# The image reloaded into dead slots of X before the barrier, corner matrices earlier, squares added on GpSimd

## What is computed

```python
x = x + gelu(layernorm_over_channels(selective_scan(groupnorm(x))) * lnw + lnb)   # "x + conv"
t = tokens(x)                                     # (4, 1024, 192)
t = t + attention(layernorm(t), qkv_w, qkv_b, proj_w, proj_b, bias_table)
t = t + experts(layernorm(t), ...)
```

## Time and profile before

| | us |
|---|---|
| median of 3 runs | 2855.5 (2854.14 to 2861.66) |
| the profiled execution | 2855.03 |
| its span in the trace | 2853.3 |
| end of `scan` (last DVE product) | 1412.84 |
| first `val` of `mid` | 1446.84 |
| last `low_part` of `mid` | 1552.12 |
| start of attention (POOL memset) | 1555.27 |

### The profile page before, as it was taken

The page is one execution under the profiler, slowest core; times in us unless marked ns, Lnnn a source line. Parts: engine busy times, 40 slices in busy tenths (PEclk is TensorE's granted clock), DMA queues, the critical chain, the costliest instruction groups (busy, mean ns, idle before and its releaser), DMA issues. The chain is left out here.

```text
span 2853.3 us, 33000 instructions
## 1 busy us (share of the span) xinstructions
PE 2263.2 (79%) x8796; PEld 805.0 (28%) x8796; DVE 2096.6 (73%) x2852; ACT 1333.5 (47%) x1870; POOL 1407.1 (49%) x726
## 2 busy tenths in 40 slices
PE   3676667665666666666678899999999879999999
PEld 1111111111111111111143123232332236766767
DVE  4999999999999999999655887786878551212212
ACT  3444445445454454445445276675767532222221
POOL 3999999999999999999545000000000110000000
PEclk9577766777676776767778799999999879999999
DMA  4544544554454445445327013112313330000000
GB/s 119 175 142 172 175 144 156 177 170 150 145 180 162 152 158 176 154 146 176 124 62 161 1 25 46 25 25 30 41 25 42 75 82 6 6 6 6 6 6 11
DMA packets 101853, 274.04 MB, mean 96 GB/s; under 512 B 17089, under 2 KB 32007, under 8 KB 101639
## 3 DMA queue, kind: packets, MB, share of 16 engines
q1 hardware_dynamic: 97600, 271.89, 32.7%
q10 hardware_dynamic: 4078, 0.19, 0.1%
HBM read 226.55 MB, written 41.22 MB: 94 GB/s over the span
## 5 line engine op out<-in xcount | busy, mean ns | idle before, releaser
L686 POOL TENSOR_TENSOR hs<-hs,c_rep 128x1024 f32<-128x1024 f32 x384 | 897.5, 2355 | 80.1 <-DVE hs L782 49.9
L472 PE MATMUL psU<-b_stack,b_sel 96*128 96x512 bf16 x640 | 312.1, 500 | 449.7 <-DVE hs L782 447.0
L1732 DVE TENSOR_REDUCE mx<-ps 128x1 f32<-128x512 f32 x864 | 539.2, 682 | 108.4 <-PE ps L1571 98.1
L1707 ACT ACTIVATE P<-ps 128x512 f32<-128x512 f32 x768 | 417.7, 599 | 239.5 <-PE ps L1583 215.4
L732 DVE TENSOR_TENSOR psU<-psU,dtu_rep 128x512 f32<-128x512 f32 x640 | 428.2, 674 | 28.5 <-PE psU L472 13.1
L601 ACT ACTIVATE decay<-dt_rep,a_neg 128x1024 f32<-128x1024 f32 x320 | 360.5, 1140 | 164.1 <-DVE hs L782 141.9
L440 PE MATMUL psY<-hs,state_sel 128*32 128x512 f32 x1572 | 424.8, 902 | 4.8 <-ACT du L578 3.5
L782 DVE TENSOR_TENSOR_SCAN hs<-decay,hs,psU 128x512 f32<-128x512 f32 x320 | 406.6, 1271 | 2.3
L782 DVE TENSOR_TENSOR_SCAN hs<-decay,psU 128x512 f32<-128x512 f32 x320 | 386.2, 1207 | 0.0
L1571 PE MATMUL ps<-ks,qs 96*128 96x512 bf16 x864 | 345.3, 403 | 24.4 <-DVE mx L1732 9.9
L472 PEld LDWEIGHTS psU<-b_stack,b_sel 96*128 96x128 bf16 x640 | 62.5, 100 | 977.8 <-DVE hs L782 875.6
(11 more groups left out here) (235 smaller groups left out, 2357.7 us busy)
## 6 DMA issues: line engine op xcount, KB each, us to landing
c_rep<-bc_rows SPq DMA_DIRECT2D x132, 512.0 KB, 4.6
dt_rep<-dt_rows SPq DMA_DIRECT2D x99, 512.0 KB, 4.5
dtu_rep<-dt_rows SPq DMA_DIRECT2D x99, 512.0 KB, 6.2
b_rep<-bc_rows SPq DMA_DIRECT2D x33, 512.0 KB, 6.0
dt_rows<-dt SPq DMA_DIRECT2D x33, 384.0 KB, 3.3
dt_rows<-soft SPq DMA_DIRECT2D x33, 384.0 KB, 3.4
qs<-qk_parts SPq DMA_DIRECT2D x90, 128.0 KB, 6.6
ks<-qk_parts SPq DMA_DIRECT2D x90, 128.0 KB, 7.2
```

The lines of the kernel that those rows point to most:

```text
L472: pe.matmul(psU[:, q % UR, :], s.b_sel[:, r, nq, :], b_stack[:, p, CH * pos:CH * pos + CH], start=True, stop=True).then_inc(b_spread, 1)
L686: pool.tensor_tensor(h, h, c_rep[:, nq, :], ALU.mult).then_inc(hc_ready, 1)
L1707: nc.scalar.activation(P[:, kt % 2, head, :], ps2[:, bank, :], ACT.Exp).then_inc(exp_done, 1)
L1732: v.reduce_max(mx[:, slot, u:u + 1], ps1[:, (slot * MAXES + u) % R, :], AX.X).then_inc(max_done, 1)
```

## The change

- `X` lives on through `mid` and `attention`. SP loads batches 0 and 1 of x into slots 1 and 2 of `X` (`raw_slot`) behind the last loads of the scan loop, in front of the barrier. `raw` and `Z` are gone: the normed batches go to slots 0 and 3 (`z_slot`).
- At the start of `mid` SP issues the table rows first, then the weights, and then batches 2 and 3 of x as soon as `add_x(0)` and `add_x(1)` have run.
- On DVE `add_x(0)` runs ahead of the copies of the projection weights; the two corner instructions run behind these copies, ahead of the first `centre`. On POOL the mask of the corners runs ahead of the first `add_squares`.
- The split of the corners moves from iteration 2 to iterations 5, 6 and 7 in pieces, the copies by SP from iteration 7 to iteration 12.
- At the end of the scan POOL adds the two halves of the squares for m = 1 to 5 (`tail_squares`: two ahead of `add_y`, three behind it), and `tail_variance` needs one matmul in place of two there.

The core of the diff (renamings of the same indices are left out):

```diff
@@ -48,6 +48,14 @@
+
+def raw_slot(b):
+    return 1 + b % 2
...
+
+def load_x(sp, w, s, b):
+    sp.dma_start(s.X[:, raw_slot(b), :, :], w.x[b].rearrange("(f p) h w -> p f (h w)", p=HC)).then_inc(s.x_in[b % 2], 16)
@@ -489,11 +497,15 @@
                 def tail_variance(m):
-                    pe.wait_ge(t_squared, m + 1)
...
                         pe.wait_ge(t_log, m - 1)
-                    for f in range(2):
-                        t = pe.matmul(psU[0:HC, m % 2, :], s.average[:], tail_work(m)[:, f, :], start=(f == 0), stop=(f == 1))
+                    if m == 0:
+                        pe.wait_ge(t_squared, 1)
+                        for f in range(2):
+                            t = pe.matmul(psU[0:HC, m % 2, :], s.average[:], tail_work(m)[:, f, :], start=(f == 0), stop=(f == 1))
+                    else:
+                        pe.wait_ge(t_summed, m)
+                        t = pe.matmul(psU[0:HC, m % 2, :], s.average[:], tail_work(m)[:, 0, :], start=True, stop=True)
@@ -715,7 +727,16 @@
                                 pool.sem_inc(alone, 1)
+                def tail_squares(m):
+                    pool.wait_ge(t_squared, m + 1)
+                    q = tail_work(m)
+                    pool.tensor_tensor(q[:, 0, :], q[:, 0, :], q[:, 1, :], ALU.add).then_inc(t_summed, 1)
+
+                tail_squares(1)
+                tail_squares(2)
                 add_y(NB * UNITS - 1, NB * UNITS // 2 - 1, NB - 1, UNITS - 1)
+                for m in range(3, TAIL_STEPS):
+                    tail_squares(m)
@@ -893,6 +914,8 @@
                         load_c(nu, 3)
+                for b in range(2):
+                    load_x(sp, w, s, b)
@@ -1025,8 +1048,6 @@
 
-        Z = sb("Zq", [HC, 2, 2, L])
-        raw = sb("raw", [HC, 2, 2, L])
@@ -1072,11 +1092,14 @@
 
-        def half(t, c, ring):
-            return t[:, c // 2 % ring, :, CH * (c % 2):CH * (c % 2) + CH]
+        def half(t, b, c):
+            return t[:, b, :, CH * (c % 2):CH * (c % 2) + CH]
+
+        def z_slot(b):
+            return 3 * (b % 2)
...
         def norm_out(kind, c):
-            return half(Z, c, 2) if kind else half(s.Y, c, NB)
+            return half(s.X, z_slot(c // 2), c) if kind else half(s.Y, c // 2, c)
@@ -1087,30 +1110,24 @@
             def _(sp):
-                def load_x(b):
-                    sp.dma_start(raw[:, b % 2, :, :], w.x[b].rearrange("(f p) h w -> p f (h w)", p=HC)).then_inc(x_in[b % 2], 16)
...
 
-                sp.dma_start(w_rows[:], w.qkvw.rearrange("(m p) d -> p m d", p=HC)).then_inc(w_in, 16)
-                load_x(0)
-                sp.dma_start(p_rows[:], w.projw.rearrange("(m p) d -> p m d", p=HC)).then_inc(p_in, 16)
...
                 sp.dma_start(hankel[:].rearrange("p e h -> p (e h)"), win).then_inc(tab_in, 16)
+                sp.dma_start(w_rows[:], w.qkvw.rearrange("(m p) d -> p m d", p=HC)).then_inc(w_in, 16)
+                sp.dma_start(p_rows[:], w.projw.rearrange("(m p) d -> p m d", p=HC)).then_inc(p_in, 16)
...
                 sp.dma_start(vb[:], w.qkvb[2 * D:3 * D].rearrange("(o d) -> o d", o=1).broadcast_to([128, D])).then_inc(vb_in, 16)
-                load_x(1)
+                for b in (2, 3):
+                    sp.wait_ge(x_added, 2 * (b - 1))
+                    load_x(sp, w, s, b)
...
                     c, m = x // MT, x % MT
-                    if i == 1:
-                        for late in (2, 3):
-                            sp.wait_ge(x_added, 2 * (late - 1))
-                            load_x(late)
@@ -1121,7 +1138,7 @@
                                 sp.dma_start(rows[19 * part:19 * part + 19, :], pick[:, k, :]).then_inc(corner_in, 16)
-                    if i == GROUPS + 1:
+                    if i == 2 * GROUPS:
@@ -1162,12 +1179,12 @@
                     add_halves(c, 1, c)
+                pool.wait_ge(corner, 2)
+                pool.affine_select(out=corners[:, 0, :, :], in_=corners[:, 0, :, :], compare_op=ALU.is_ge, fill=0.0, base=0,
+                                   pattern=[[0, HEADS], [1, 19]], channel_multiplier=-1).then_inc(corner, 1)
...
                 add_halves(2, 1, 2)
-                pool.wait_ge(corner, 2)
-                pool.affine_select(out=corners[:, 0, :, :], in_=corners[:, 0, :, :], compare_op=ALU.is_ge, fill=0.0, base=0,
-                                   pattern=[[0, HEADS], [1, 19]], channel_multiplier=-1).then_inc(corner, 1)
@@ -1319,16 +1336,17 @@
                 def add_x(b):
-                    v.wait_ge(x_in[b % 2], 16 * (b // 2 + 1))
+                    v.wait_ge(s.x_in[b % 2], 16 * (b // 2 + 1))
...
                     for c in range(2):
-                        y = half(s.Y, 2 * b + c, NB)
-                        v.tensor_tensor(y, half(raw, 2 * b + c, 2), y, ALU.add).then_inc(x_added, 1)
+                        y = half(s.Y, b, c)
+                        v.tensor_tensor(y, half(s.X, raw_slot(b), c), y, ALU.add).then_inc(x_added, 1)
...
                 v.memset(scl[:, 2:3], 1.0).then_inc(own_v, 1)
+                add_x(0)
@@ -1336,7 +1354,12 @@
                 t.then_inc(padded, 1)
-                add_x(0)
+                v.wait_ge(tab_in, 16)
+                v.wait_ge(last_in, 16)
+                v.tensor_copy(corners[:, 0, :, :], hankel[:].rearrange("p e h -> p h e")[:, :, ::-1]).then_inc(corner, 1)
+                v.wait_ge(corner, 1)
+                v.tensor_tensor(corners[:, 0, :, :], corners[:, 0, :, :], last_row[:].unsqueeze(2).broadcast_to([19, HEADS, 19]),
+                                ALU.subtract).then_inc(corner, 1)
@@ -1344,12 +1367,6 @@
                 t.then_inc(w_taken, 1)
-                v.wait_ge(tab_in, 16)
-                v.wait_ge(last_in, 16)
-                v.tensor_copy(corners[:, 0, :, :], hankel[:].rearrange("p e h -> p h e")[:, :, ::-1]).then_inc(corner, 1)
-                v.wait_ge(corner, 1)
-                v.tensor_tensor(corners[:, 0, :, :], corners[:, 0, :, :], last_row[:].unsqueeze(2).broadcast_to([19, HEADS, 19]),
-                                ALU.subtract).then_inc(corner, 1)
@@ -1381,16 +1398,16 @@
                         add_x(LAST)
-                    if i == 2:
-                        for part in range(QPART):
-                            m = v.tensor_copy(corner_parts[:, :, part, :, :], corners[:])
-                            if part == QPART - 1:
-                                m.then_inc(corner_split, 1)
-                            else:
-                                own(m)
-                                own.wait()
-                                own(v.tensor_tensor(corners[:], corners[:], corner_parts[:, :, part, :, :], ALU.subtract))
-                                own.wait()
+                    if 5 <= i < 5 + QPART:
+                        part = i - 5
+                        m = v.tensor_copy(corner_parts[:, :, part, :, :], corners[:])
+                        if part == QPART - 1:
+                            m.then_inc(corner_split, 1)
+                        else:
+                            own(m)
+                            own.wait()
+                            own(v.tensor_tensor(corners[:], corners[:], corner_parts[:, :, part, :, :], ALU.subtract))
+                            own.wait()
@@ -2052,10 +2069,12 @@
         s.ext = nc.dram_tensor("table_twice", (37, HEADS), F32, kind="Internal").ap()
+        held_x = ExitStack()
+        s.X = held_x.enter_context(nc.sbuf_tensor("X", [HC, NB, 2, L], F32))
+        s.x_in = [held_x.enter_context(nc.semaphore(f"x_again{i}")) for i in range(2)]
...
                 return c2.enter_context(nc.sbuf_tensor(name, shape, dt))
-            s.X = sb2("X", [HC, NB, 2, L])
@@ -2078,6 +2097,7 @@
             attention(nc, w, s)
+        held_x.close()
```

More of the change, by code:

```diff
@@ L340, in scan @@
         t_mean, t_centred, t_squared, t_var = sem("t_mean"), sem("t_centred"), sem("t_squared"), sem("t_var")
-        t_log, t_dev, t_normed = sem("t_log"), sem("t_dev"), sem("t_normed")
+        t_log, t_dev, t_normed, t_summed = sem("t_log"), sem("t_dev"), sem("t_normed"), sem("t_summed")
         TAIL_STEPS = 2 * NORMED_IN_SCAN
@@ L1053, in mid @@
             sem("w_in"), sem("vb_in"), sem("qb_in"), sem("p_in"), sem("tab_in"), sem("last_in"))
-        x_in = [sem(f"x_again{i}") for i in range(2)]
         both_ready, mean_ready, centred, squared = sem("both_ready"), sem("mean_ready"), sem("centred"), sem("squared")
@@ L1147, in add_halves @@
                         pool.wait_ge(x_added, c + 1)
-                    y = half(s.Y, c, NB)
+                    y = half(s.Y, c // 2, c)
                     pool.tensor_tensor(work[:, n % NORMS, 0, :], y[:, 0, :], y[:, 1, :], ALU.add).then_inc(both_ready, 1)
@@ L1234, in _ @@
                             t = pe.matmul(ps_w[:, i % RING, :], w_qkv[:, h, 128 * m:128 * m + 128],
-                                          Z[:, b % 2, h, CH * c:CH * c + CH], start=(h == 0), stop=(h == 1))
```

(5 more changed lines are left out.)

## The result

The changed kernel took 2839.16 us (median of 6 runs, 2838.25 to 2843.51) where the kernel before took 2857.29 on the same chip (6 runs, 2854.14 to 2861.66): a ratio of 0.9938, 95% interval 0.9925 to 0.9950, or 17.7 us less (14 to 21). The forecast of 2837.5 lies 1.7 us off; as a change it was 17.5 us less, and the sign and the range hold. The sum inside it does not hold in every term, as the milestones show. The profiled execution of the changed kernel was the slowest of the six (2843.51, span 2841.7), so the same kernel was profiled again (`e1_again`, span 2830.3), and both traces are read side by side. Of the six runs of `e1_again` one took 3369.09 us at a granted clock of 0.616 and is left out here; the median of the other five is 2834.54.

What follows compares the result with a forecast made beforehand. The barrier-bounded middle stage was taken to set the span one for one: waiting holes first, then full PE and DMA. Terms 1.4 - 5.8 - 4.9 - 6.7 - 1.5 = -17.5 from 2855.03 gave 2837.5 us, range 2828.5 to 2846.5.

Steps and rivals of the forecast that it cites:

- Part 1: Scan's end: fewer matmuls, but DVE and GpSimd block each other and PE idles; 1.4 us lost, bounds 0.6 gained, 2.4 lost.
- if variance 3 were slow as well: Scan's end, outer bound: variance 3's matmuls also slow and more DVE-GpSimd blocks come; 2.4 us lost.
- Part 2: Front of the middle stage: add_x(0) awaits only the gelu, so everything up to the first centre moves by -5.8 us.
- the half us to spare: Front of the middle stage: slack with which the corner subtraction is covered ahead of centre; uncovered it costs 0.6 to 1.5 us.
- Part 3: First projection: early corner mask frees PE, then the three-column product holds the first val; -4.9 us, bounds 0 and -8.
- Part 4: Iterations 0 to 4: x wait and corner split go, 13.7 us, less 7.0 for new blocks; -6.7, bounds -2 and -11.
- Part 5: Iterations 5 to 23: full DMA stretch begins 3 us sooner without the corner copies ahead; -1.5 us, bounds 0 and -3.
- against a DMA backlog that is then still small: Iteration 12: the moved corner copies put SP 2.6 us behind, while little DMA work is queued.
- warm pipeline: Rival: PE stays at full clock in all three old slow stretches, 5 to 8 us more gained, 2831 us; chance 0.22.
- Blocks close the gaps: Rival: DVE and GpSimd meet in nearly every new gap, only about 10.5 us gained, 2844.5 us; chance 0.21.
- Hidden anyway: Rival: the full DMA engines fix the end of the middle stage's second half, time stays at 2855 us; chance 0.03.
- lock step: Rival: every subtraction falls behind two GpSimd operations, 20 more at 2.2 us each, 2881.5 us; chance 0.02.

Runs made afterwards that it cites:

- e7_padded: Kernel before plus eight increments of an unused semaphore on DVE at the middle stage's start; 2855.32 us, ratio 0.9987.
- e8_best: Changed kernel with GpSimd additions only for m = 1 and 2, corner copies in iteration 19, three-column product ahead of the first scaling; 2828.76 us, ratio 0.9896.
- e3_corners_late: Changed kernel with the six corner copies moved from iteration 12 to iteration 19; 2839.35 us, ratio 0.9930.
- e10_corners_at_7: Same as e8_best but with the corner copies in iteration 7, as in the kernel before; 2827.15 us, ratio 0.9874.
- e5_x_only: Kernel before with only x loaded early and add_x(0) ahead of the weights, corners and scan's end unchanged; 2849.47 us, ratio 0.9962.

## Why the prediction was right, and where it was not

**What bounds the kernel.** The reading held: the middle stage's milestones moved, and the span with them. That "whatever shortens the middle stage shortens the span one for one" missed two things: the stages behind can change on their own, and the end of the middle stage can take back a shift from its front, as the 3.2 us in `e7_padded`.

**Part 1, forecast +1.4.** Measured +2.2 and +2.5 with the change, +1.8 alone. That is at the bound of +2.4. The step that failed is that DVE would sit under GpSimd's additions until 1406.1. It lasted 1.46 us and the additions waited. What was left over from that is PE: idle for 2.43 us, then at the lower clock level for variances 3 and 4 (3.70 in place of 1.9) and not for variance 5 alone. The case "if variance 3 were slow as well" was a bound and should have been the value: the idleness of PE in front of variance 3 was counted in the prediction (3.6 us in all), and its price was laid on the last matmuls alone. The section that the prediction weighs (the Trainium skill, SBUF — State Buffer, "Who interferes with whom") also says: "Issue order, not op shape, decides who blocks." The 1.46 of DVE, which started 0.32 us ahead of the additions, agrees, and the prediction had not used it. The 2.89 of the earlier trace rows does not: there DVE's subtraction started 1.20 us ahead of the second GpSimd operation and waited for it as well.

**Part 2, forecast -5.8.** Measured -5.7 and -5.6 (`centre` at 8.08 and 8.10, not 13.74). Each step stands in the trace: `add_x(0)` 2.5 us after the start (forecast 2.4), loads landed, the corner subtraction covered. But the half us to spare was gone: the weight copies, stretched under `add_halves`, filled it.

**Part 3, forecast -4.9.** From `centre` to the first `val` the gain was a further 2.6 us in one trace and 5.0 in the other. The wait that was named, the three columns, is the one that ended last (4.70 <- DVE), in both. The 2.4 between them go with the clock of PE in the stage ahead: the kernel before had its variance at the upper level (1.10), the first trace at the lower (2.02). At the upper level the forecast was right. `e8_best` shows the wait's worth: without it 3 us more are gained, in line with the bound of -8.

**Part 4, forecast -6.7.** From the first `val` to that of iteration 4 the kernel took 23.37 us before and 12.91 and 11.59 after: -10.5 and -11.8, near the bound of -11 and beyond it. The wait for x went, as forecast, and blocks took its place, but they were mis-sized. The forecast had one subtraction of over 4 us and 1.6 on the scaling, 6.3 in all; measured were 2.72, 2.34, 2.17 and 1.48 in place of 0.69, 0.69, 1.22 and 0.69, 5.4 of DVE's time. The forecast took 7.0 off the 13.7, and the rows tell most of what was wrong with that. The `val` of iteration 4 started at 1456.10, while the second subtraction ran and ahead of the scaling (2.17) and the last one (1.48), and so it was in `e1_again`. So at most 3.7 us of the four (2.03 of the first, 1.65 of the second) lay ahead of this milestone, and 13.7 - 3.7 = 10.0 is close to the measured 10.5. The step that failed is the size of the block on the subtraction of iteration 2 (4.7 forecast, 2.0 measured) and the 1.6 on a scaling that comes only behind the milestone. Then iterations 4 to 8 took 23.42 in both traces, not 21.46: +2.0, the upper end of what was set for the corner pieces. The pieces are not its cause, for with the corner part alone that stretch took 21.45, and with x alone, without the pieces, 24.61. It belongs to the new phase between the engines; what in it, stays open. The two stretched instructions behind the `val` of iteration 4 are 1.7 of DVE's time there, and no experiment was made on them. To iteration 8 the sum is -8.5 and -9.8.

**Part 5, forecast -1.5.** Measured +3.0 and +1.9 from iteration 8 to attention's start (63.60 before, 66.56 and 65.52 after). The step that failed is "against a DMA backlog that is then still small". The copies in iteration 12 are followed by a wait of 5.58 us on a store, and `e3_corners_late`, without them there, brings the term to -0.1. But `e8_best` has them in iteration 19 as well and took 65.5, `e10_corners_at_7` took 64.0: terms of +1.9 and +0.4. So the price of the copies in iteration 12 lies between nothing and 3 us and is not settled closer. Of the kernels with a part of the change in this stage only `e5_x_only` gained anything in this stretch (62.7), and the kernel before with idle increments took 60.3. So the hoped-for gain of 1.5 is not seen, and a term of this size can't be read from one trace.

**What was not in the sum.** The stages behind the middle one gave 2.4 and 7.3 us, by the experiments some 6 as a mean, most of it through the stalls of DVE at the loop's turns. The forecast came out near the measured 17.7 because this gain and that of iterations 0 to 4 made up for parts 1 and 5. That the sum met the measured time to 1.7 us is luck; that parts 2, 3 and 4 pay, and that their waits are the ones named, is not.

**The rivals.** The warm pipeline is seen in part: `e1_again` has the upper clock level in the front, and the shorter middle stage; the other traces with this front do not. "Blocks close the gaps" came true in their number (nine long subtractions, not four) and not in their price, since iterations 0 to 4 gained more than forecast. The last sign that the prediction named was many more than 4 subtractions over 2 us; there were six. "Hidden anyway" is wrong for the whole, since the stack loads moved with iteration 8, but `e7_padded` shows that the end of the stage can hide some 3 us. The lock step did not come: 15 of 24 subtractions stayed at 0.69.

## What to carry to other kernels

Work that is shifted onto an idle engine is worth its cost only where the engine that is relieved stays busy: two additions ahead of `add_y` gained some 2 us, three more behind it lost some 4, through waits and through PE's clock after them. A small instruction on which the next stage waits goes to the head of its queue (three columns, 3 us). Small copies in a queue in which stores gate an engine can delay that engine: here by 5 us at iteration 18, of which some 2 were given back by the end of the stage. Measure the stages that were not edited as well: 2.4 of 11.6 and 7.3 of 23.0 us came from them in the two pairs of traces, and eight idle instructions did the same.

## What the runs showed of the hardware

- An instruction that waited on the shared port of DVE and GpSimd did not always lose. At the earlier trace rows DVE's subtraction waited for two GpSimd operations (2.89 us); at the scan's end DVE, started 0.37 us before `add_y` ended, went first, and the additions took 3.48 in place of 2.54. What decides between the two was not settled.
- The position of code changes DVE's stalls at the turns of attention's loop: longest 4.8 to 4.9 us in three traces and 2.4 to 2.7 in nine, with 111 packets on the instruction queue against 109 or 110. The Trainium skill (Runtime: NRT & Kernel Launch, "Instruction fetch mechanics") says that an engine holds two blocks of its code, that blocks are loaded by DMA, and that a taken branch out of them stalls until the target's block is there. The rows agree with it: the stalls stand at loop turns, eight idle instructions change them, and two packets fewer are on the instruction queue. Which block boundary moved was not looked at, so the mechanism is argued and only the dependence on placement is shown.
- The two matmuls of one variance took 2.02 and 1.10 us in two executions of the same kernel, and the middle stage 128.3 and 123.6. Three more traces with the same front had 2.02.
- A DVE instruction of three columns took 0.24 us alone and 1.22 while GpSimd ran `add_halves`; two copies of 96x192 float32 took 0.24 to 0.26 and, under the same, 0.96 and 1.25.
- The scan's loop itself, unchanged in all kernels, ended between 1383.3 and 1388.2 us. This scatter is more than most of the terms that are discussed here, so they were read from milestones inside each trace.
